# Halves of q and k turned 32 columns at a time, four side by side, in an attention and mixture-of-experts layer

## The chip, the cores and the metric

The kernel runs on one core of a Trainium2 chip. The metric is the device time of the program in microseconds; lower is better. Engines are named as the profile names them: PE is TensorE, DVE is VectorE, ACT is ScalarE, POOL is GpSimd, SP is SyncE, which only issues DMAs here.

## The reference

The input is x, 8 sequences of 512 tokens of 256 features. One layer is computed:

```python
x = layernorm(x + attention(x))
x = layernorm(x + ffn(x))

# attention: 16 heads of 16
qkv = x @ w_qkv.T                       # q, k, v
q, k = rms_norm(q) * q_w, rms_norm(k) * k_w
q, k = rope(q, k)                       # halves of each head rotated by cos, sin
attn = softmax(causal(q @ k.T) * 16 ** -0.5)
out = (attn @ v) @ w_proj.T

# ffn: a shared expert and the best 2 of 8 experts, 256 -> 1024 -> 256
normed = rms_norm(x) * norm_weight
shared = relu(normed @ sw1 + sb1) @ sw2 + sb2
routed = sum over the best two of w_e * (relu(normed @ ew1[e] + eb1[e]) @ ew2[e] + eb2[e])
```

## The kernel before

Each engine runs its own program, in order; semaphores are all that ties them together. The attention half is one long list of steps `g` from -40 to 209, the same for all engines: a job of batch `c` (one sequence) stands at step 20 c plus an offset from a table at the top of the file (`QK`, `ROPE`, `QN`, `TR`, `V`, `AV`, `NAT`, `PROJ` and so on), and the first two batches have offsets of their own (`OPENING`). Within a step each engine takes its jobs in the order in which its function `step` lists them. So in any stretch of 20 steps the scores of batch c run beside the preparation of q and k of batch c + 2 and the projection, norms and routing of batch c - 1. Below, "position 6 of a batch" is a step with g = 6 modulo 20, and "position 106" is g = 106. A tile is 128 tokens; a batch has four.

Products of two 32-bit values are made of 16-bit pieces: a value is a high part and a low part. For the scores each head's 16 columns of q stand in the contraction as high, low, high, low and those of k as high, low, low, high, 64 rows in all, so that one product of 64 rows gives all four pairs. The path of one tile of q and k is:

- TensorE makes q and k (L1681, position `QK`) and ScalarE copies them and their squares (L885, L888).
- GpSimd's `swap` (L696, L699) and VectorE's `rope` and `summed` (L1153, L1168) rotate them; VectorE's `normed` scales them into `qn` (L1183, position `QN`).
- One position later GpSimd's `nat_high` writes the high part into `nat` (L707); for the first batch ScalarE does it (`first_high`, L893). Two positions after `QN` VectorE's `nat_low` writes the low part (L1193).
- Three positions after `QN` GpSimd's `nat_twice` copies the two halves a second time, straight for q (L714) and with its parts swapped for k (L715), each as 256 words of 32 bits.
- At position `TR` (6, 10, 14 and 18 of a batch for tiles 0 to 3) TensorE's `stacked` turns the 64 columns of two heads at once: 8 turns of 128 columns for q into bank `ma` (L1691), 8 for k into bank `mc` (L1697). A turn is a matmul with the identity as the moving operand, 128 columns. ScalarE copies each bank into `stk` (L982, L985), from which the scores are made.

TensorE's order within a step is: scores and causal masks of two units (L1642, L1655), on even positions; `stacked`; `QK`; `V`; `NAT`, the attended rows turned back, tile t at positions 4, 6, 8, 10 (L1806); `AT` at 12 and 16 (L1706); `PROJ`, the projection, at 14 and 18 (L1818); `XN`, `LG`, `RANK`, the router's parts; `AV`, the pv products, at 1, 6, 11 and 16 (L1668). The pv products are already 32 columns wide and four side by side, each in a quarter of the array's columns. The scores use 64 rows, all else the full array.

`NAT` and `PROJ` share the bank `mb`: tile t + 1 of `NAT` waits for VectorE's L1202, which reads tile t out of it, and `PROJ` waits for `aT`, ScalarE's copy of the turned rows (L1003). VectorE's `added` reads the projection (L1220), makes the variance, and GpSimd's `norms` waits for that (L723). GpSimd also issues the scatters, indirect DMAs that write rows to DRAM by expert (L740, offsets `SPACED`). The next batch's x is split into high and low parts by ScalarE at position `SPLIT_X` (L1020) and VectorE one position later (L1452).

Of the kernel before, what the change touches and what calls it, by code (L numbers as in the profile page):

```python
# [8 lines left out]
ACT = mybir.ActivationFunctionType  # L9
AX = mybir.AxisListType  # L10
F32 = mybir.dt.float32
F16 = mybir.dt.float16
# [5 lines left out]
NB, T, D = 8, 512, 256  # L18
NH, HD = 16, 16
# [61 lines left out]
QN = (-20, -18, -12, -10)  # L81
TR = (-14, -10, -6, -2)
# [15 lines left out]
SPACED = (58, 60, 62, 66)  # L98
# [3 lines left out]
SPLIT_X = (-33,)  # L102
# [42 lines left out]
def due(offsets, g):  # L145

    return [(c, i) for i in range(len(offsets)) for c in range(NB) if position(offsets, c, i) == g]
# [99 lines left out]
def program(nc, a, S, keep):  # L247

    with ExitStack() as ctx:
# [80 lines left out]
        ma = ps("ma", T)  # L330
# [3 lines left out]
    with ExitStack() as ctx:  # L334
# [81 lines left out]
        def halves(n):  # L416

            if n in (2, 3):
                return prob[:, 1, n - 2, 0:1024].bitcast(F16).rearrange("p (k h d) -> p k h d", k=2, h=NH)
            return nat[:, n % 2]  # L420

        def halves_words(n):

            if n in (2, 3):
                return prob[:, 1, n - 2, 0:1024].rearrange("p (k h d) -> p k h d", k=2, h=NH)
            return nat[:].bitcast(F32)[:, n % 2]

# [47 lines left out]
        with nc.Block() as block:  # L475
# [176 lines left out]
            def _(pool):  # L652
# [56 lines left out]

                def nat_twice(n):  # L710

                    pool.wait_ge(S("nat_lo"), n + 1)
                    q, k = halves_words(n)[:, 0], halves_words(n)[:, 1]
                    pool.tensor_copy(q[:, :, HD:2 * HD], q[:, :, 0:HD]).then_inc(S("nat_ready"), 1)  # L714
                    pool.tensor_copy(k[:, :, HD:2 * HD].rearrange("p h (s d) -> p h s d", s=2),  # L715
                                     k[:, :, 0:HD].rearrange("p h (s d) -> p h s d", s=2)[:, :, ::-1, :]
                                     ).then_inc(S("nat_ready"), 1)
# [53 lines left out]
                def step(g):  # L771
                    for c, t in due(QN, g - 3):
                        nat_twice(4 * c + t)
# [62 lines left out]
            def _(act):  # L836
# [53 lines left out]
                def first_high(n):  # L890

                    act.wait_ge(S("qn_done"), n + 1)
                    act.activation(halves(n)[:, :, :, 0:HD].rearrange("p k h d -> p (k h) d"),  # L893
                                   qn[:, n % 2, :].rearrange("p (h d) -> p h d", d=HD), ACT.Copy).then_inc(S("nat_hi"), 1)

# [721 lines left out]
            def _(pe):  # L1617
# [67 lines left out]
                def stacked(c, t):  # L1685

                    n = 4 * c + t
                    pe.wait_ge(S("nat_ready"), 2 * (n + 1))
                    pe.wait_ge(S("ma_free"), NTH["tq", c, t])
                    for i in range(8):  # L1690
                        last = pe.transpose(ma[:, 64 * i:64 * i + 64].bitcast(F16),  # L1691
                                            halves(n)[:, 0, 2 * i:2 * i + 2, :].rearrange("p h d -> p (h d)"), ident_h[:])
                    last.then_inc(S("tq_done"), 1)
                    if NTH["tk", c, t]:
                        pe.wait_ge(S("mc_free"), NTH["tk", c, t])
                    for i in range(8):
                        last = pe.transpose(mc[:, 64 * i:64 * i + 64].bitcast(F16),  # L1697
                                            halves(n)[:, 1, 2 * i:2 * i + 2, :].rearrange("p h d -> p (h d)"), ident_h[:])
                    last.then_inc(S("tk_done"), 1)
# [77 lines left out]
                def step(g):  # L1777
# [9 lines left out]
                    for c, t in due(TR, g):  # L1787
                        stacked(c, t)
# [44 lines left out]
                    for c, _ in due(RANK, g):  # L1833
# [12 lines left out]
                        last.then_inc(S("rank_done"), 1)  # L1846
                    for c, i in due(AV, g):
                        attended(c, i)
# [188 lines left out]
```

## Time and profile before

| | |
|---|---|
| time, median of 3 runs | 947.77 us (946.87 to 948.3) |
| the profiled execution | 947.38 us, its span 945.6 us |
| PE busy | 882.1 us, 93% of the span |
| ACT busy | 614.4 us, 65% |
| DVE busy | 583.0 us, 62% |
| POOL busy | 438.7 us, 46% |
| mean granted clock of PE | 0.98 of full |
| L714, 28 copies in `nat` between 36 and 330 us | 20.9 us, mean 747 ns |
| L715, 28 copies in `nat` between 36 and 330 us | 14.4 us, mean 515 ns |

Positions 0, 20, 40, ... 140 begin at 36.13, 80.81, 122.59, 163.71, 205.44, 249.40, 290.64 and 328.70 us, read off the start of the first scores of each batch. Busy time is the union of an engine's instructions; "idle before" is the time in which the engine had nothing to run, with the instruction that ended it. The ends of matmuls are modelled, so a matmul of 128 columns is shown as 0.22 us though the next one starts some 0.06 us after it: in a row of eight the start of the next group tells the pace. Durations in the rows are of one profiled execution.

### The profile page before, as it was taken

Reading aid. Unit: us, or ns where it says so; the run is one execution under the profiler, and the core shown is the slowest. Engines: PE = TensorE matmul, PEld = TensorE weight load, DVE = VectorE, ACT = ScalarE, POOL = GpSimd, SP = SyncE. Lnnn points to the kernel's source line nnn. Section 1 sums busy time; section 2 is a strip of 40 time slices with the busy share of each in tenths; the row PEclk is TensorE's granted clock in tenths of the full one; section 3 lists DMA queues with packets and bytes.
Section 4 is the critical chain, followed back from the end, with each engine's and each line's share of the span. In section 5 each row is a group of like instructions: output and inputs, shape, how many; then the busy total and the mean of one; then the engine's idle time right before and its main releaser. Section 6 shows DMA issues by size and latency. Waiting matters only on the chain.

```text
span 945.6 us, 26104 instructions
## 1 busy us (share of the span) xinstructions
PE 882.1 (93%) x9049; PEld 699.2 (74%) x9050; DVE 583.0 (62%) x1206; ACT 614.4 (65%) x1061; POOL 438.7 (46%) x602
## 2 busy tenths in 40 slices
PE   3778999998999989999999999999999999999997
PEld 1444556565655646888889989989899989898886
DVE  8664778998888747784444444454444432437986
ACT  4678889887987866442656655556655454666774
POOL 5352555878777646572135444343434344421321
PEclk8799999999999999999999999999999999999999
DMA  5112242425312156567882122121212111238751
GB/s 177 68 68 68 68 146 90 139 100 184 108 70 75 61 181 217 210 209 268 273 283 78 52 62 69 54 67 52 72 45 79 46 58 47 70 114 286 233 168 55
DMA packets 68705, 112.76 MB, mean 119 GB/s; under 512 B 7728, under 2 KB 46000, under 8 KB 68496
## 3 DMA queue, kind: packets, MB, share of 16 engines
q1 hardware_dynamic: 51248, 77.32, 24.8%
q10 hardware_dynamic: 10896, 16.40, 5.8%
q0 software_dynamic: 6480, 17.97, 5.2%
q8 instruction: 50, 0.82, 0.4%
q14 instruction: 31, 0.25, 0.1%
HBM read 66.58 MB, written 45.08 MB: 118 GB/s over the span
## 4 chain that ended last, share of the span: by engine, by line
PE 64%; POOL 11%; ACT 9%; issue 9%; DVE 3%; DMA 2%; another core or an unknown queue 1%; ACTq 0%; DVEq 0%; POOLq 0%; SPq 0%
PE yb L1903 24%; PE hb L1884 24%; ACT prob L871 4%; PE pv_bank L1668 4%; PE hb L1734 3%; POOL xg_rows L740 2%; PE slot L1642 1%; PE tr L1754 1%; POOL rsum L699 1%; PE ma L1681 1%; POOL rsum L696 1%; POOL vv L723 1%; POOL nat L707 1%; PE yb L1771 1%
## 5 line engine op out<-in xcount | busy, mean ns | idle before, releaser
L1043 ACT ACTIVATE hf<-hb,b 128x256 f32<-128x256 f32 (+1 forms) x392 | 154.8, 453 | 201.1 <-PE hb L1884 182.5
L1884 PE MATMUL hb<-xgT,wts 128*128 128x256 f16 (+1 forms) x1872 | 213.3, 263 | 1.5 <-ACT hf L1043 1.3
L1903 PE MATMUL yb<-wts,hh 128*128 x1704 | 210.5, 273 | 0.7 <-DVE hh L1472 0.6
L1472 DVE TENSOR_TENSOR hh<-hf,hh 128x1024 f16<-128x1024 f32 (+1 forms) x98 | 119.9, 1227 | 132.9 <-ACT hh L1048 105.0
L1884 PEld LDWEIGHTS hb<-xgT,wts 128*128 x1872 | 181.2, 98 | 20.7 <-ACT hf L1043 1.1
L806 POOL DMA_INDIRECT y_tok<-yb,dest x71 | 77.7, 1095 | 229.0 <-DVE yb L1484 212.2
L1903 PEld LDWEIGHTS yb<-wts,hh 128*128 128x128 f16 x1704 | 166.4, 98 | 19.4 <-DVE hh L1472 0.9
L871 ACT ACTIVATE prob<-slot 128x1024 f32<-128x1024 f32 x160 | 156.1, 1037 | 31.9 <-PE slot L1655 29.9
L1048 ACT ACTIVATE hh<-hf 128x1024 f16<-128x1024 f32 (+1 forms) x98 | 97.6, 996 | 3.1
L740 POOL DMA_INDIRECT xg_rows<-xnh,sl_i x64 | 78.3, 1224 | 15.5 <-issue 13.2
L1484 DVE SCALAR_TENSOR_TENSOR yb<-yb,b2bc 128x512 f32<-128x512 f32 (+1 forms) x39 | 25.1, 643 | 85.2 <-PE yb L1903 84.0
L1668 PE MATMUL pv_bank<-prob,vst 128*32 128x512 f32 (+3 forms) x1024 | 76.6, 440 | 0.5 <-ACT prob L871 0.5
L1642 PE MATMUL slot<-stk 64*128 64x128 f16 (+3 forms) x512 | 53.6, 303 | 23.2 <-ACT prob L871 16.5
L1681 PE MATMUL ma<-wqkv,xTh 128*128 128x256 f16 (+1 forms) x348 | 65.0, 333 | 9.1 <-ACT raw L888 3.8
L1668 PEld LDWEIGHTS pv_bank<-prob,vst 128*32 128x32 f32 x1024 | 30.0, 110 | 45.4 <-issue 35.5
L1642 PEld LDWEIGHTS slot<-stk 64*128 64x128 f16 x512 | 18.0, 94 | 49.6 <-ACT prob L871 27.3
L1681 PEld LDWEIGHTS ma<-wqkv,xTh 128*128 128x128 f16 x348 | 34.0, 100 | 27.5 <-issue 6.3
L1884 PE MATMUL hb<-xgT,wts_s 128*128 128x256 f16 x480 | 54.0, 273 | 0.0
L1903 PE MATMUL yb<-wts_s,hh 128*128 128x256 f16 x456 | 51.3, 273 | 0.0
L1884 PEld LDWEIGHTS hb<-xgT,wts_s 128*128 128x128 f16 x480 | 47.0, 98 | 5.4
L723 POOL TENSOR_TENSOR vv<-vv,keep_mhalf 128x4 f32<-128x4 f32 x16 | 21.5, 1345 | 62.2 <-DVE vv L1239 62.2
L1903 PEld LDWEIGHTS yb<-wts_s,hh 128*128 128x128 f16 x456 | 44.6, 98 | 5.2
(250 smaller groups left out, 1441.6 us busy)
## 6 DMA issues: line engine op xcount, KB each, us to landing
wts<-in_w_all SPq DMA_DIRECT2D x23, 512.0 KB
wts<-y_tok SPq DMA_DIRECT2D x32, 256.0 KB, 4.9
xg<-xg_rows ACTq DMA_DIRECT2D x30, 264.0 KB, 2.7
stage<-in_w_all SPq DMA_DIRECT2D x12, 512.0 KB
w_split<-chunk_hl SPq DMA_DIRECT2D x12, 512.0 KB
xTf<-in_xT SPq DMA_DIRECT2D x8, 512.0 KB, 4.4
xin<-in_x SPq DMA_DIRECT2D x8, 512.0 KB, 4.1
resid<-y SPq DMA_DIRECT2D x16, 256.0 KB
```

Source lines behind the costliest of these rows:

```text
L723: pool.tensor_tensor(vv[:, pair(u), 4:6], vv[:, pair(u), 0:2], mhalf[:].unsqueeze(1).broadcast_to([P, 2, 2]), ALU.pow).then_inc(S("norms_r ...
L740: pool.indirect_dma_start(a["xg_rows"], bass.IndirectOffsetOnAxis(ap=sl_i[:, c % 2, t, k:k + 1], axis=0), xnh[:, c % 2, t, :], None).then_ ...
L806: pool.indirect_dma_start(a["y_tok"], bass.IndirectOffsetOnAxis(ap=dest[:, slot, j:j + 1], axis=0), yb[:, par, j, :], None).then_inc(S(f"y ...
L871: act.activation(dst, src, ACT.Exp, scale=ATT_SCALE).then_inc(S("exp_done"), 1)
L1043: act.activation(hf[:, c, 0:size], hb[c // 2][:, (c % 2) * TT:(c % 2) * TT + size], ACT.Relu, bias=bias, scale=1.0 / WS).then_inc(S("relu_ ...
L1048: act.activation(hh[:, par, 0, cs, 0:size], hf[:, cs, 0:size], ACT.Copy).then_inc(S("h_hi"), 1)
L1472: dve.tensor_tensor(hh[:, par, 1, cs, 0:size], hf[:, cs, 0:size], hh[:, par, 0, cs, 0:size], ALU.subtract).then_inc(S("h_lo"), 1)
L1642: pe.matmul(slot[:, 512 * x + col:512 * x + col + T - P * j], stk[rows, par, 1, pr, P * j:P * j + P], stk[rows, par, 0, pr, P * j:T], star ...
L1668: last = pe.matmul(pv_bank[32 * r:32 * r + 32, P * j:T], vst[:, c % 2, j, 4 * g + r, :], prob[:, g % 2, r, SEG[j]:SEG[j] + T - P * j], sta ...
L1681: last = pe.matmul(out, xTh[:, c % 2, x, k, P * t:P * t + P], wqkv[:, y, k, cols], start=(n == 0), stop=(n == len(pieces) - 1))
L1884: ins = pe.matmul(hb[hc // 2][:, (hc % 2) * TT:(hc % 2) * TT + size], weights(e, c, w, hc * P, P), xgT[:, par, x * DC + c, 0:size], start= ...
L1903: ins = pe.matmul(bank, hh[:, par, x, hc, P * j:P * j + P], weights(e, DC + hc * D // CH, w, hc * D % CH, D), start=(n == 0), stop=(n == H ...
```

## The change

`nat_twice` goes. Instead the high part of k is written a second time, behind its low part, so that a head of k holds high, low, high: by GpSimd behind `nat_high`, by ScalarE behind `first_high` for the first batch. `stacked` no longer turns 64 doubled columns of two heads at once but 32 columns at a time into a quarter of the partitions, four such matmuls to a block: for q high and low of a head, twice; for k columns 0 to 31 (high, low) and 16 to 47 (low, high). It is moved in TensorE's step from behind the masks to ahead of the pv products. The third scatter of a batch's first four goes from offset 62 to 64, and the split of x from -33 to -34.

```diff
--- before.py
+++ after.py
@@ -95,11 +95,11 @@
 RANK = (56,)
 SCATTER = (58, 59, 61, 63)
 SCATTER_2 = (64, 66, 67, 68)
-SPACED = (58, 60, 62, 66)
+SPACED = (58, 60, 64, 66)
 SPACED_2 = (67, 68, 70, 72)
 STORE = (39, 43)
 STORE_XT = (43, 49)
-SPLIT_X = (-33,)
+SPLIT_X = (-34,)
 LOAD_XIN = (20,)
 LOAD_XT = (-51,)
 UNITS = tuple(range(NPOS))
@@ -419,12 +419,6 @@
                 return prob[:, 1, n - 2, 0:1024].bitcast(F16).rearrange("p (k h d) -> p k h d", k=2, h=NH)
             return nat[:, n % 2]
 
-        def halves_words(n):
-
-            if n in (2, 3):
-                return prob[:, 1, n - 2, 0:1024].rearrange("p (k h d) -> p k h d", k=2, h=NH)
-            return nat[:].bitcast(F32)[:, n % 2]
-
         def rotated(n):
 
             return prob[:, 1, n, 0:2 * D] if n in (2, 3) else rsum[:, n % 2, :]
@@ -706,15 +700,8 @@
                     pool.wait_ge(S("tk_done"), n - 1)
                     pool.tensor_copy(nat[:, n % 2, :, :, 0:HD].rearrange("p k h d -> p (k h) d"),
                                      qn[:, n % 2, :].rearrange("p (h d) -> p h d", d=HD)).then_inc(S("nat_hi"), 1)
-
-                def nat_twice(n):
-
-                    pool.wait_ge(S("nat_lo"), n + 1)
-                    q, k = halves_words(n)[:, 0], halves_words(n)[:, 1]
-                    pool.tensor_copy(q[:, :, HD:2 * HD], q[:, :, 0:HD]).then_inc(S("nat_ready"), 1)
-                    pool.tensor_copy(k[:, :, HD:2 * HD].rearrange("p h (s d) -> p h s d", s=2),
-                                     k[:, :, 0:HD].rearrange("p h (s d) -> p h s d", s=2)[:, :, ::-1, :]
-                                     ).then_inc(S("nat_ready"), 1)
+                    pool.tensor_copy(nat[:, n % 2, 1, :, 2 * HD:3 * HD],
+                                     qn[:, n % 2, D:2 * D].rearrange("p (h d) -> p h d", d=HD)).then_inc(S("nat_again"), 1)
 
                 def norms(c, u):
 
@@ -769,8 +756,6 @@
                                            ).then_inc(S("x1_done"), 1)
 
                 def step(g):
-                    for c, t in due(QN, g - 3):
-                        nat_twice(4 * c + t)
                     for c, t in due(QN, g - 1):
                         if c >= 1:
                             nat_high(4 * c + t)
@@ -892,6 +877,9 @@
                     act.wait_ge(S("qn_done"), n + 1)
                     act.activation(halves(n)[:, :, :, 0:HD].rearrange("p k h d -> p (k h) d"),
                                    qn[:, n % 2, :].rearrange("p (h d) -> p h d", d=HD), ACT.Copy).then_inc(S("nat_hi"), 1)
+                    act.activation(halves(n)[:, 1, :, 2 * HD:3 * HD],
+                                   qn[:, n % 2, D:2 * D].rearrange("p (h d) -> p h d", d=HD), ACT.Copy
+                                   ).then_inc(S("nat_again"), 1)
 
                 def roots(c, u):
 
@@ -1685,17 +1673,24 @@
                 def stacked(c, t):
 
                     n = 4 * c + t
-                    pe.wait_ge(S("nat_ready"), 2 * (n + 1))
+                    pe.wait_ge(S("nat_lo"), n + 1)
+                    pe.wait_ge(S("nat_again"), n + 1)
                     pe.wait_ge(S("ma_free"), NTH["tq", c, t])
+
+                    def turned(bank, i, r, rows):
+
+                        return pe.matmul(bank[32 * r:32 * r + 32, 64 * i:64 * i + 64].bitcast(F16), rows, ident_h[:],
+                                         is_transpose=True)
+
                     for i in range(8):
-                        last = pe.transpose(ma[:, 64 * i:64 * i + 64].bitcast(F16),
-                                            halves(n)[:, 0, 2 * i:2 * i + 2, :].rearrange("p h d -> p (h d)"), ident_h[:])
+                        for r in range(4):
+                            last = turned(ma, i, r, halves(n)[:, 0, 2 * i + r // 2, 0:2 * HD])
                     last.then_inc(S("tq_done"), 1)
                     if NTH["tk", c, t]:
                         pe.wait_ge(S("mc_free"), NTH["tk", c, t])
                     for i in range(8):
-                        last = pe.transpose(mc[:, 64 * i:64 * i + 64].bitcast(F16),
-                                            halves(n)[:, 1, 2 * i:2 * i + 2, :].rearrange("p h d -> p (h d)"), ident_h[:])
+                        for r in range(4):
+                            last = turned(mc, i, r, halves(n)[:, 1, 2 * i + r // 2, HD * (r % 2):HD * (r % 2) + 2 * HD])
                     last.then_inc(S("tk_done"), 1)
 
                 def rows_turned(bank, rows, u):
@@ -1784,8 +1779,6 @@
                                 scores(c, k)
                             for k in (p, p + 1):
                                 masked(k)
-                    for c, t in due(TR, g):
-                        stacked(c, t)
                     for c, t in due(QK, g):
                         if c >= 1:
                             pe.wait_ge(S("xT_lo"), c + NT)
@@ -1844,6 +1837,8 @@
                                              msum[:, i, :].unsqueeze(1).broadcast_to([P, NT, NE]),
                                              start=False, stop=(i == NT - 1), skip_group_check=True)
                         last.then_inc(S("rank_done"), 1)
+                    for c, t in due(TR, g):
+                        stacked(c, t)
                     for c, i in due(AV, g):
                         attended(c, i)
                     for kind, m, q in early_due(g):
```

## Rows read from the trace of the kernel before

**Rows 1.** Busy time of each engine in 249.40 to 290.60 us (windows), with counts.

```profile
249.40:290.60 41.20, 38.96 (x456) 24.12 (x456) 36.48 (x94) 35.29 (x56) 30.81 (x37) 1.00 0.27 94
```

**Rows 2.** Waits of TensorE, 80.8 to 328.7 us: us in total, times, longest.

```profile
PE slot L1642 <- ACT prob L871: 6.9, 16, 1.2
PE ma L1691 <- POOL nat L715: 4.1, 4, 1.4
```

**Rows 3.** Timeline of TensorE, positions 100 to 120: start, length, line, [idle before <-releaser].

```profile
261.53 0.62 PE L1691 MATMUL ma<-keep_ident,nat 128*128 128x128 f16 x8 [0.58 <-POOL nat L715]
261.99 0.61 PE L1697 MATMUL mc<-keep_ident,nat 128*128 128x128 f16 x8
...
268.81 0.39 PE L1642 MATMUL slot<-stk 64*128 64x512 f16 x2 [0.20 <-ACT prob L871]
269.72 0.39 PE L1642 MATMUL slot<-stk 64*128 64x128 f16 x4 [0.52 <-ACT prob L871]
...
270.39 0.61 PE L1691 MATMUL ma<-keep_ident,nat 128*128 128x128 f16 x8
...
278.66 0.61 PE L1691 MATMUL ma<-keep_ident,nat 128*128 128x128 f16 x8
...
287.64 0.61 PE L1691 MATMUL ma<-keep_ident,nat 128*128 128x128 f16 x8
```

**Rows 4.** Timeline of TensorE, the turn of tile 0 in the two batches before.

```profile
176.61 0.62 PE L1691 MATMUL ma<-keep_ident,nat 128*128 128x128 f16 x8 [1.35 <-POOL nat L715]
...
218.36 0.62 PE L1691 MATMUL ma<-keep_ident,nat 128*128 128x128 f16 x8 [1.38 <-POOL nat L715]
```

**Rows 5.** Copies on GpSimd, 36 to 330 us: busy us, mean ns | idle before.

```profile
L714 POOL COPY nat<-nat 128x256 f32<-128x256 f32 x28 | 20.9, 747 | 25.5 <-DVE nat L1193 25.3 <-issue 0.2
...
L715 POOL COPY nat<-nat 128x256 f32<-128x256 f32 x28 | 14.4, 515 | 0.0
```

**Rows 6.** Timeline of VectorE, positions 101 to 110.

```profile
257.46 1.89 DVE L1193 TENSOR_TENSOR nat<-qn,nat 128x512 f16<-128x512 f32 x1 [0.28 <-POOL nat L707]
...
261.20 0.42 DVE L1202 TENSOR_TENSOR an<-mb,rcp 128x256 f32<-128x256 f32 x1
...
267.42 0.69 DVE L1168 TENSOR_TENSOR rsum<-rot,rsum 128x512 f32<-128x512 f32 x1 [0.85 <-POOL rsum L699]
...
270.82 0.42 DVE L1202 TENSOR_TENSOR an<-mb,rcp 128x256 f32<-128x256 f32 x1
```

**Rows 7.** Timeline of VectorE beside the two turns of rows 4.

```profile
176.62 0.42 DVE L1202 TENSOR_TENSOR an<-mb,rcp 128x256 f32<-128x256 f32 x1
...
217.70 0.42 DVE L1202 TENSOR_TENSOR an<-mb,rcp 128x256 f32<-128x256 f32 x1
```

**Rows 8.** Timeline of ScalarE, positions 107 to 120.

```profile
266.80 1.04 ACT L1020 ACTIVATE xTh<-xTf 128x1024 f16<-128x1024 f32 x1
...
278.36 0.65 ACT L1003 ACTIVATE aT<-mb 128x512 f32<-128x512 f32 x1
...
289.92 0.62 ACT L985 ACTIVATE stk<-mc 128x512 f32<-128x512 f32 x1
```

**Rows 9.** VectorE groups, 36 to 330 us: busy us, mean ns | idle before.

```profile
L1193 DVE TENSOR_TENSOR nat<-qn,nat 128x512 f16<-128x512 f32 x28 | 23.1, 825 | 8.1 <-POOL nat L707 7.9
...
L1452 DVE TENSOR_TENSOR xTh<-xTf,xTh 128x1024 f16<-128x1024 f32 x6 | 7.4, 1226 | 0.2
```

**Rows 10.** Timeline of TensorE's weight loads in and behind the pv products.

```profile
220.26 0.13 PEld L1668 LDWEIGHTS pv_bank<-prob,vst 128*32 128x32 f32 x4 [0.30 <-issue]
220.69 0.13 PEld L1668 LDWEIGHTS pv_bank<-prob,vst 128*32 128x32 f32 x4 [0.30 <-issue]
...
222.09 0.33 PEld L1642 LDWEIGHTS slot<-stk 64*128 64x128 f16 x8 [0.20 <-issue]
```

**Rows 11.** The page, part 5: the weight loads of the pv products: busy us, mean ns.

```profile
L1668 PEld LDWEIGHTS pv_bank<-prob,vst 128*32 128x32 f32 x1024 | 30.0, 110 | 45.4 <-issue 35.5
```

**Rows 12.** TensorE's sequencer at line L1804, 261 to 263 us.

```profile
L1804 PEldq EVENT_SEMAPHORE  x1: 51/51/51, 261.7 to 261.7; - x1
```

## The prediction, made blind

> **What bounds the kernel now.** I read the page first, then the same stretch four times over: TensorE's waits in it, and the timelines of TensorE, VectorE, ScalarE and GpSimd side by side. The page's slices show TensorE at nine tenths through the second half of the span: the feed-forward half, behind the attention, is matmuls back to back, and nothing that the change touches runs there. So the change can act only in the attention half, and whatever it wins or loses by position 140 (328.7 us) is carried to the end. There a batch lasts some 41 us, and in the one that I follow, positions 100 to 119, TensorE is busy 38.96 of 41.20 us, ScalarE 35.29, VectorE 36.48, GpSimd 30.81 [rows 1]. The reader is to see that four engines run nearly full, with TensorE nearest its limit: a wait removed on GpSimd is worth at most what TensorE waits.
>
> TensorE's own waits from position 20 to 140 are the budget of the argument [rows 2]: 4.1 us in 4 waits for GpSimd's doubling copies, 6.9 us in 16 waits for an exponential to free a scores bank. The first kind sits at one place, the turn of tile 0 at position 6 of a batch (0.58 us in the batch that I follow [rows 3]; 1.35 and 1.38 two and one batches earlier [rows 4]). At position 10 the scores wait 0.20 and 0.52 us [rows 3].
>
> **The copies removed.** GpSimd loses 32 pairs, of 747 and 515 ns on average, and gains 28 copies of a quarter of q and k's values; the nearest row is the second removed copy, 515 ns, which I take, so a batch has 4 x (1.26 - 0.52) = 3.0 us less GpSimd work [rows 5]. That alone is worth nothing: what counts is who waits. For tile 0 that is TensorE, 4.1 us in all [rows 2]. For VectorE it is the sum of the next tile (0.85 us [rows 6]), late because the copies stood ahead of GpSimd's swap.
>
> **What takes the wait's place.** The turn no longer stands ahead of the attended rows' turns (L1806) and of the projection (L1818), but behind them. At position 6 the attended tile 1 needs the bank from VectorE's L1202 on tile 0. That ends at 261.62, while the doubling copies let TensorE go at 261.53 [rows 3, 6]: the new wait ends 0.09 us later than the old one. In the two batches of [rows 4, 7] L1202 ends at 177.04 and 218.12 against 176.61 and 218.36. From the end of the scores TensorE would then wait 1.35 + 0.43 = 1.8, 1.38 - 0.24 = 1.1, 0.58 + 0.09 = 0.7, and in batch 6, which has the remaining 0.8 of the 4.1 us, some 0.9: 4.5 us in place of 4.1. Behind the waiting instruction TensorE has the turn, the pv products and the next scores queued, and ScalarE's exponentials wait for those. Against it, the projection is no longer behind the turn at positions 14 and 18, so VectorE's sums, GpSimd's norms and the tile's start on VectorE come earlier, by up to the 0.9 us that two half turns take (8 turns in 0.46 us [rows 3]). GpSimd is not idle before it, so I credit 0.5 us in each of four batches: 2.0 us.
>
> **The split of x one position earlier.** ScalarE's 1.04 us (L1020 at 266.80 [rows 8]) stood behind the copy that waits for the pv products and ahead of the exponentials of position 8; it now runs while ScalarE would wait for pv. It can take at most 1.04 us from the waits of position 10; in the batch followed there are 0.20 + 0.52 = 0.72, and five batches have such a split: 3.6 us (bounds 0 and 5.2). But VectorE's half (L1452, 1226 ns [rows 9]) moves too, from behind to ahead of its L1202 on tile 2, which ended at 271.24 where TensorE began the turn of tile 1 at 270.39 [rows 3, 6]. With the attended turn first, TensorE wants that bank at 270.39 - 0.72 = 269.67 and gets it at 271.24 + 1.23 - 0.85 (the wait of VectorE that goes) - 0.5 = 271.12: 1.4 us. In the other four batches VectorE is further ahead; I take 0.3 each: 2.6 us in all (bounds 0 and 5 x 1.4 = 7.0).
>
> **The turns moved behind the projection.** At position 14 the turn began at 278.66, and the projection, which now comes first, needs ScalarE's aT, done at 279.01 [rows 3, 8]. The turn used to cover this: 0.35 us and some 0.03 for the semaphore, six times: 2.3 us. At position 18 the scores of the next batch wait for ScalarE's copy of the turned k, begun at 289.92 [rows 8]. The turn began at 287.64 [rows 3]. Now 12 matmuls of 256 columns go first, 1.37 us at 57 ns for 128; with a change of array shape (0.1, below), two half turns (0.92) and the tail of the last (0.16) k is turned at 290.2, some 0.2 us after ScalarE wanted it: six times 0.2, 1.2 us. Position 14 also gets a change between full-width and 32-column matmuls that was not there. The load behind pv starts after a gap of 0.20 us [rows 10]; between nothing and that I take 0.1, six times: 0.6 us. Positions 6 and 10 have pv next, so none is added.
>
> **The turns themselves.** 16 turns of 128 columns become 64 of 32, four side by side. Two things could make them dearer. First the pace of a group of four: in pv the loads of a set of four stand 0.43 us apart (220.26, 220.69) for 512 fp32 columns, that is 0.107 for 128, and a 16-bit turn streams in half that time: 8 turns in 0.46 us, 57 ns each [rows 3, 10]. Four loads of 110 ns are over in 0.13 us, so they start within 0.02 us [rows 10, 11]. So a group of four should take the time of one full turn and I charge nothing; the other bound is a whole load of 110 ns [rows 11] for each group in place of 57 ns: 53 ns more x 16 groups x 28 tiles = 24 us. Second the instructions: 96 more a tile, 3,072 in all. After the wait ended at 261.53, TensorE's sequencer was past all 32 instructions of a turn by 261.7 [rows 3, 12], some 5 ns each, while the new turns need 128 in 0.9 us, 7 ns each: hidden. The Trainium skill has a figure against the change: "TensorE: Matmul & The Clock Gate", section LDWEIGHTS, gives the load as columns / 1.2 ns, 27 ns for 32 columns, 107 ns if the four of a group followed one another; its section Back-to-back issue gap has a floor of some 25 ns for a matmul, 100 ns for four. By either a tile costs about 0.8 us more, an estimate; pv's loads and matmuls, 0.02 us for four, disagree [rows 10].
>
> **The opening.** The tiles of the first batch wait for the copies too, but the last of them waits for VectorE's work on tiles 2 and 3, which does not change, and ScalarE gets four more copies ahead of its own copies of the turned tiles. I set it at 0, between one pair of copies won and as much lost, 1.3 us [rows 5]. The scatter moved from position 62 to 64 goes behind the high part of tile 1 in GpSimd's queue, and its DMA with it; its rows are read only after the attention half, and with the copies gone nothing of TensorE waits behind it: 0.
>
> **Sum.** Won: 4.1 + 3.6 + 2.0 = 9.7. Lost: 4.5 + 2.6 + 2.3 + 1.2 + 0.6 = 11.2. Net 1.5 us slower. The profiled execution took 947.38 us (945.6 of span), 0.4 under the median of the runs, 947.77; I add the sum to the median: **949.3 us**. This measurement can tell some 0.2%, 1.9 us, from no change.
>
> **Rivals.** (A) *VectorE is freed and the new waits vanish: faster.* Its L1193 on tile 0 lasted 1.89 us beside GpSimd, against 825 ns on average [rows 6, 9]. If less GpSimd work gives it 1.2 us back, L1202 comes that much earlier, the wait at position 6 falls from 4.5 - 2.0 = 2.5 to nothing and that at position 10 from 2.6 to nothing: 1.5 - 5.1 = -3.6 us, 944.2, and with the upper bound of the split of x, 5.2 for 3.6, 942.6. For it: every term on VectorE is short of its limit by a microsecond or less. Against: the removed copies ran mostly when VectorE's durations were normal. It decides as soon as VectorE gains 0.6 us a batch. (B) *VectorE's chain gets longer: slower.* The new copy stands on GpSimd straight ahead of the swap, where L1193 was held 1.2 us. If it is held 0.5 us longer, the credit of 2.0 goes and both waits grow, 6 x 0.4: 1.5 + 2.0 + 2.4 = 5.9 us, 953.7. It decides if L1193 at position 2 lasts over 2 us. (C) *The loads of a group are not hidden:* 24 us more, 975; against it speaks pv. The skill's figures would give the same, 0.8 x 28 = 22 us, an estimate.
>
> **Chances.** Forecast (946 to 952) 0.36, of it 0.06 faster, 0.20 the same, 0.10 slower; A 0.32, faster; B 0.22, of it 0.04 the same; C 0.10, slower. So faster 0.38, same 0.24, slower 0.38. The range leaves out C and the far ends of A: 941 to 959; the forecast's own is 946 to 952.
>
> **What would show it.** Right: L1691's waits for GpSimd gone; L1806 at position 6 waiting for VectorE, L1818 at position 14 for ScalarE, some 0.4 us; a half turn of 32 matmuls in 0.45 to 0.5 us; position 20 to 140 lasting 248 to 251 us against 247.9. Wrong: those waits at zero (A), L1193 at 2 us or more (B), a half turn of 0.8 us or more (C), or a wait on the turn itself for VectorE's low part, which I have at nothing.

## The result and the profile after

The kernel after takes 953.58 us (median of 5 runs, 951.71 to 954.25) against 947.77 (946.87 to 948.3): 1.0051 of before, 95% interval 1.0031 to 1.0071, so slower, by 4.8 us at that ratio. Its profiled execution took 953.96 us against 947.38. The 6.6 us between the two lie where the prediction looked: from position 20 to 140 the attention half lasts 253.5 us (82.53 to 336.00) in place of 247.9, 1.7 us more come up to position 20, and behind position 140 it is 0.7 us less.

The batches from 164.60, from 207.94 and from 252.00 us, the last to be read against [rows 1] (start:end, length, busy us of PE, PEld, DVE, ACT, POOL, granted clock):

```profile
252.00:297.20 45.20, 40.98 (x648) 25.47 (x649) 38.16 (x99) 35.68 (x56) 28.10 (x36) 0.96 0.24 82
207.94:252.00 44.06, 40.57 (x648) 25.30 (x649) 38.68 (x91) 37.45 (x58) 29.93 (x34) 0.96 0.38 125
164.60:207.94 43.34, 39.42 (x649) 24.38 (x650) 39.09 (x100) 36.53 (x57) 29.67 (x35) 1.00 0.39 127
```

GpSimd is relieved as the change wants (28.10 us busy for 30.81), and yet the batch followed in the prediction takes 4.0 us longer: TensorE is busy 2.0 us more, at 0.96 of its clock, and idle 2.0 us more. VectorE is busy 1.7 us more, though its program is the same.

Waits of TensorE, 82.5 to 336 us, to be read against [rows 2]:

```profile
PE slot L1630 <- ACT prob L856: 6.3, 12, 1.6
PE mb L1799 <- DVE an L1190: 4.5, 5, 1.8
PE slot L1630 <- ACT stk L970: 3.4, 4, 0.9
PE mb L1811 <- ACT aT L991: 2.4, 6, 1.1
PE slot L1630 <- ACT stk L973: 1.8, 1, 1.8
PE mc L1682 <- issue: 0.9, 2, 0.5
PE slot L1630 <- issue: 0.8, 1, 0.8
```

The wait for the doubling copies is gone; the attended rows wait for VectorE and the projection for ScalarE instead, as forecast. The scores at the six batch starts from position 20 to 120 wait 6.0 us in all (3.4 and 1.8 for ScalarE's copies of the turned rows, 0.8 at 164.60 for nothing that the profile names) in place of 5.1. Timeline of TensorE in the batch of [rows 3]:

```profile
263.71 0.63 PE L1799 MATMUL mb<-ident_f,raw 128*128 128x128 f32 x4 [0.16 <-DVE an L1190]
264.27 0.63 PE L1682 MATMUL ma<-keep_ident,nat 128*32 128x128 f16 x32
264.73 0.82 PE L1682 MATMUL mc<-keep_ident,nat 128*32 128x128 f16 x32
...
274.39 1.08 PE L1799 MATMUL mb<-ident_f,raw 128*128 128x128 f32 x4 [1.82 <-DVE an L1190]
275.41 1.04 PE L1682 MATMUL ma<-keep_ident,nat 128*32 128x128 f16 x32
276.24 1.07 PE L1682 MATMUL mc<-keep_ident,nat 128*32 128x128 f16 x32
...
284.34 1.48 PE L1811 MATMUL mb<-wproj,aT 128*128 128x256 f16 x12 [0.27 <-ACT aT L991]
285.76 0.63 PE L1682 MATMUL ma<-keep_ident,nat 128*32 128x128 f16 x32
286.21 0.62 PE L1682 MATMUL mc<-keep_ident,nat 128*32 128x128 f16 x32
286.77 0.61 PE L1630 MATMUL slot<-stk 64*128 64x128 f16 x6
```

32 narrow turns stand 0.46 us apart (264.27, 264.73), as 8 wide ones did. Behind the wait of 1.82 us at position 10 the half turns take 0.83 and 0.85: the clock has fallen, as the two windows below show, one over that place and one ten microseconds earlier (granted clock third from the right):

```profile
274.00:277.40 3.40, 3.01 (x72) 2.58 (x76) 3.19 (x9) 1.09 (x2) 1.56 (x3) 0.51 0.09 30
264.00:267.40 3.40, 3.40 (x98) 2.06 (x97) 3.30 (x4) 3.40 (x6) 3.21 (x4) 1.00 0.14 43
```

0.51 is the 1.2 GHz level, 1.00 the 2.4 GHz one; TensorE had been idle 1.8 us just before. VectorE shows what made that wait; compare [rows 6]:

```profile
259.14 2.22 DVE L1181 TENSOR_TENSOR nat<-qn,nat 128x512 f16<-128x512 f32 x1 [0.28 <-POOL nat L701]
...
272.39 1.22 DVE L1440 TENSOR_TENSOR xTh<-xTf,xTh 128x1024 f16<-128x1024 f32 x1
...
273.82 0.42 DVE L1190 TENSOR_TENSOR an<-mb,rcp 128x256 f32<-128x256 f32 x1
```

VectorE's half of the split of x now stands ahead of L1190 on tile 2, so L1190 ends at 274.24, and the low part, beside GpSimd's second copy and its swap, lasts 2.22 us in place of 1.89.

What was not forecast is at position 6 and after. In the batch before the one above, TensorE, then ScalarE, then GpSimd:

```profile
220.93 2.33 PE L1656 MATMUL pv_bank<-prob,vst 128*32 128x512 f32 x32
...
228.47 0.39 PE L1630 MATMUL slot<-stk 64*128 64x512 f16 x2 [1.62 <-ACT prob L856]
...
231.31 1.04 PE L1682 MATMUL ma<-keep_ident,nat 128*32 128x128 f16 x32
```

```profile
222.19 1.14 ACT L1008 ACTIVATE xTh<-xTf 128x1024 f16<-128x1024 f32 x1
225.15 0.60 ACT L861 ACTIVATE raw<-pv_bank 128x512 f32<-128x512 f32 x1 [1.81 <-remote]
...
227.41 1.92 ACT L856 ACTIVATE prob<-slot 128x1024 f32<-128x1024 f32 x2
```

```profile
221.65 1.01 POOL L727 DMA_INDIRECT xg_rows<-xnh,sl_i  x1 [0.17 <-issue]
222.96 0.96 POOL L727 DMA_INDIRECT xg_rows<-xnh,sl_i  x1 [0.30 <-issue]
224.23 1.02 POOL L727 DMA_INDIRECT xg_rows<-xnh,sl_i  x1 [0.30 <-issue]
```

The pv products of position 6 end at 223.26. ScalarE's copy of them, L861, waits for nothing else, and yet starts at 225.15, as the third of three scatters on GpSimd ends (225.25). The profile names no instruction of this core as the releaser ("remote"). The trace's record of the semaphore says the same: its update stands at 225.12, 1.87 us behind the end that the profile gives the pv products. The masks behind them, by their rows over at 224.12 and 224.34, are released at 225.92, while TensorE goes on starting a matmul every 0.11 us. The exponentials queued behind the copy are then late, the scores of position 10 wait 1.62 us, and the next turns run at half clock. In the kernel before the scatters started 2.1 to 2.2 us behind the pv products.

What this costs can't be read off this batch, since the kernel before waits and falls to half clock at the same place. Its TensorE, and a window there (granted clock third from the right):

```profile
226.59 0.39 PE L1642 MATMUL slot<-stk 64*128 64x512 f16 x2 [1.15 <-ACT prob L871]
```

```profile
228.50:231.90 3.40, 3.40 (x26) 2.10 (x26) 3.37 (x5) 2.72 (x4) 3.23 (x2) 0.50 0.34 122
```

The batch lasts 44.06 us after and 43.96 before. Of the 5.6 us that positions 20 to 140 grew by, 4.0 lie in the batch from 252.00 us, with the wait of 1.82 us for VectorE and the half clock behind it, which the kernel before doesn't have there.

### The profile page after: what moved, and what is told of

It is laid out like the page before. It is cut to its first block, busy times and chain, and to the rows that moved or that the text cites. A ratio compares the mean times of both kernels' runs of the same rounds, so it can differ in the third digit from the quotient of the medians.

```text
span 952.2 us, 29144 instructions
## 1 busy us (share of the span) xinstructions
PE 887.7 (93%) x10585; PEld 701.9 (74%) x10586; DVE 587.1 (62%) x1206; ACT 616.6 (65%) x1065; POOL 410.4 (43%) x566
## 4 chain that ended last, share of the span: by engine, by line
PE 68%; ACT 10%; DVE 7%; issue 6%; POOL 4%; DMA 2%; another core or an unknown queue 1%; ACTq 0%; DVEq 0%; SPq 0%; POOLq 0%
PE yb L1898 24%; PE hb L1879 24%; PE pv_bank L1656 5%; ACT prob L856 5%; PE hb L1729 3%; PE slot L1630 2%; PE ma L1669 2%; PE slot L1643 2%; PE mb L1811 1%; PE tr L1749 1%; DMA rs<-resid 1%; PE yb L1766 1%; PE ma L1682 1%; DVE nat L1181 1%
## 5 line engine op out<-in xcount | busy, mean ns | idle before, releaser
L727 POOL DMA_INDIRECT xg_rows<-xnh,sl_i x64 | 74.5, 1164 | 15.4 <-issue 12.8
L701 POOL CAST nat<-qn 128x512 f16<-128x512 f32 x28 | 22.9, 818 | 61.1 <-DVE qn L1171 58.2
```

The lines of the kernel that those rows point to most:

```text
L727: pool.indirect_dma_start(a["xg_rows"], bass.IndirectOffsetOnAxis(ap=sl_i[:, c % 2, t, k:k + 1], axis=0), xnh[:, c % 2, t, :], None).then_ ...
```

## The experiments

Twelve kernels, each timed in five rounds beside the kernel before on the same chip: e1 to e4 on one chip, f1 to f4 on a second, g1 to g4 on a third. Results are ratios to the kernel before of the same rounds, with 95% intervals; the quotient of two of them is known to some 0.2 to 0.35%. Five theories came up, three at first: O, the order of the turns costs; S, the earlier split pays; W, narrow turns cost (called P with f1 to f4); and later V, the second copy of k's high parts holds VectorE; C, the scatter's place matters. The first four kernels take away the order, the split, both, or everything else.

**e1, the turns ahead again.** The kernel after, with:

```
+                    for c, t in due(TR, g):
+                        stacked(c, t)
                     for c, t in due(QK, g):
...
-                    for c, t in due(TR, g):
-                        stacked(c, t)
                     for c, i in due(AV, g):
```

> The changed kernel with the turns back at their old place in TensorE's step (behind the masks, ahead of the attended rows' turns and the projection); 32-column turns, no doubling copies, the split of x and the scatter as changed. Theory O (the order costs: TensorE stands at the attended turn for VectorE and at the projection for ScalarE's aT): the 4.5 and 2.4 us of those waits go, so it is 5 to 8 us faster than the changed kernel, 945.5 to 948.5, and the waits for L1190 and L991 vanish from TensorE's list. Theory S (the split of x is what costs, by VectorE's half ahead of L1190): within 2 us of the changed kernel, 952 to 955. Theory W (the 32-column turns themselves are dearer than they look): within 2 us of the changed kernel too.

**e2, the split at -33** (`-SPLIT_X = (-34,)`, `+SPLIT_X = (-33,)` in the kernel after).

> The changed kernel with the split of x back at -33, nothing else. Theory S: VectorE's 1.23 us is again behind its L1190 on tile 2, the wait of 1.82 us at position 10 falls under 0.7, 3 to 5 us faster than the changed kernel, 949 to 951. Theory O: the waits for L1190 shrink but the exponentials of position 8 come 1 us later, within 2 us of the changed kernel, 952 to 955.

**e3, both of these edits.**

> Both taken back: the turns ahead and the split of x at -33; what is left of the change is the 32-column turns, the copies gone and the scatter at 64. Theory W: still 3 us or more slower than the kernel before, over 951. Theories O and S: nothing waits for the doubling copies (4.1 us) any more and no new wait is added, so 2 to 4 us faster than the kernel before, 944 to 946.

**e4, only the order.** The kernel before, wide turns and doubling copies, with the first diff the other way round.

> The kernel before, with full-width turns and the doubling copies, and only the turns moved behind the projection, ahead of the pv products. Theory O: 4 to 8 us slower than the kernel before, 952 to 956, with TensorE's waits for L1202 and aT. Theories S and W: within 1.5 us of the kernel before.

Measured: e1 1.0071 (1.0045 to 1.0097), e2 1.0063 (1.0043 to 1.0083), e3 1.0130 (1.0095 to 1.0164), e4 0.9979 (0.9961 to 0.9997). So theory O falls: the order alone is worth 2 us (e4), and with narrow turns and without the doubling copies it is worth 0.67% (e3 over e2). The split is nearly neutral beside pv (e2) and pays 0.6% where the turns stand ahead (e3 over e1). What costs is in the turns or the copies. Theories O and S forecast 944 to 946 us for e3; it is the slowest kernel of all, 960.97.

**f1, narrow turns over doubled columns.** e4 with:

```
                     for i in range(8):
-                        last = pe.transpose(ma[:, 64 * i:64 * i + 64].bitcast(F16), ...)
+                        for r in range(4):
+                            last = turned(ma, i, r, halves(n)[:, 0, 2 * i + r // 2, 2 * HD * (r % 2):2 * HD * (r % 2) + 2 * HD])
...
```

and the same for k into `mc`.

> e4_only_moved (turns behind the projection, split of x and scatter as before) with the turns 32 columns wide, but taken from the doubled layout: GpSimd's doubling copies stay and there is no second high copy. It tells the width alone. Theory P (the narrow turns cost on TensorE: two more changes of array shape a batch, more instructions, a lower clock): 3 to 8 us slower than e4_only_moved. Theory V (the cost lies in GpSimd's new copy, which stands where VectorE writes the low part, 165 ns longer on average in the changed kernel): within 2 us of e4_only_moved.

**f2, the second copy later.** e2, with GpSimd's second copy taken out of `nat_high` into a function of its own, `nat_again`, and:

```
                 def step(g):
+                    for c, t in due(QN, g - 3):
+                        if c >= 1:
+                            nat_again(4 * c + t)
```

> e2_split_later (the changed kernel with the split of x at -33) with GpSimd's second copy of k's high part two positions later, where the doubling copies stood. Theory V: VectorE's low part is no longer held beside it (1022 ns on average back to some 860), 4 us or more faster than e2_split_later. Theory P: within 2 us of e2_split_later.

**f3, the scatter back.** e2 with `SPACED = (58, 60, 62, 66)`.

> e2_split_later with the scatter back at offset 62 from 64. A third theory, C: the scatter at 64 stands ahead of the swap of tile 2 and makes it late, with it VectorE's sum and all behind: then 3 us or more faster than e2_split_later. Theories P and V: within 2 us of it.

**f4, one copy more.** e4 with the second high copy beside the doubling copies.

> e4_only_moved with full-width turns and the doubling copies, and GpSimd's second copy of k's high part added behind the first (it is overwritten by the doubling copy later, so nothing is changed in the output). Theory V: the low part lasts over 1000 ns on average and it is 3 to 7 us slower than e4_only_moved. Theory P: within 2 us of e4_only_moved; in both GpSimd has 0.4 to 0.6 us more a tile.

Measured: f1 1.0015 (0.9997 to 1.0033), f2 1.0039 (1.0021 to 1.0058), f3 1.0115 (1.0087 to 1.0144), f4 0.9996 (0.9980 to 1.0012). The narrow turns cost 0.36% (f1 over e4), as theory P had it. The copy as an extra costs 0.17%, though it lengthens the low parts to 945 ns from 830 on average; moved later (f2 under e2) it gives 0.24% back; both are within the intervals and under what theory V forecast. Theory C went the other way round: scatter 64 saves 0.5% (e2 under f3), where every theory had f3 within 2 us of e2, or faster. And there is a gap: f1 and f3 differ only in the copies, GpSimd's work from position 0 to 140 is 167.1 us in f3 against 185.4, and f3 is 1.0% slower.

The last four kernels are the fourth corner of the square {wide, narrow} x {doubled, second copy}, a kernel half way, and two that start from e4.

**g1, wide turns with the second copy.** f3 with the turns of before:

```
-                        for r in range(4):
-                            last = turned(ma, i, r, ...)
+                        q = halves(n)[:, 0, 2 * i:2 * i + 2, :].rearrange("p h d -> p (h d)")
+                        last = pe.transpose(ma[:, 64 * i:64 * i + 64].bitcast(F16), q, ident_h[:])
```

It leaves the mixed products of high and low parts out of the scores, since the columns that would hold the doubled halves are zero; GpSimd writes these zeros once at the start.

> The fourth corner of a square: turns wide or narrow, by doubling copies or by the second copy of k's high parts, all with the turns beside pv, the split of x at -33 and the scatter at 62. Three corners are measured: wide and doubled 0.9979 of before, narrow and doubled 1.0015, narrow and second copy 1.0115. This one has the second copy and turns 128 columns at a time again, which read columns that are zero in place of the doubled ones, so what it computes of q and k is wrong; GpSimd zeroes those columns once at the start. Theory W, the narrow turns' instructions on TensorE are late in supply and hold up its semaphores where turns and pv stand side by side (in the kernel after, pv_done at position 6 comes 0.65 to 1.87 us after the end that its records give, with nothing else released in between): without them those late updates go, and the time falls to 0.996 to 1.000 of before (944 to 949 us), 12 to 15 us under the narrow one. Theory G, the second copy holds VectorE up (its low parts take 965 to 1022 ns in the place of 859) and that is what costs the 9.5 us between narrow doubled and narrow second copy: the time stays at 1.006 to 1.010 (955 to 958 us). If the two simply add: 1.0115 less 0.0036 is 1.008, 957 us.

**g2, only k narrow** (g1 with k's loop of four; the same products are left out, since q's doubled columns are zero).

> As the one before, q turned wide (reading zeros in the doubled columns, so its result is wrong), k turned 32 columns at a time: half of the extra instructions. Theory W: if the supply runs out only past some density, this is near the wide one (0.997 to 1.002 of before) and pv_done at position 6 is on time; if each extra instruction costs alike, halfway between the wide one and 1.0115. Theory G: as the wide one, 1.006 to 1.010, since the copies are the same.

**g3, e4 with** `SPACED = (58, 60, 64, 66)`.

> The kernel before with the turns beside pv and the third scatter at 64. The scatter at 62 cost 0.5% in the narrow kernel (5 us). If that holds for the wide one too, 0.992 to 0.994 of before (941 to 943 us); if it mattered only because GpSimd's second copy stands there, 0.998, as the turns moved alone.

**g4, g3 with** `SPLIT_X = (-34,)`.

> The kernel before with all of the change but the narrow turns and the copies: turns beside pv, the third scatter at 64, the split of x at -34. The split was worth 0.1% (unclear) beside pv and 0.6% ahead. Expected 0.991 to 0.997 of before (940 to 946 us), under both kernels; it would be at or over 0.998 if scatter and split are worth something only beside the second copy.

Measured: g1 1.0067 (1.0054 to 1.0081), g2 1.0077 (1.0063 to 1.0090), g3 0.9956 (0.9941 to 0.9971), g4 0.9990 (0.9980 to 0.9999). The square, in per cent of before:

| | doubling copies | second copy |
|---|---|---|
| wide | e4 -0.21 | g1 +0.67 |
| narrow | f1 +0.15 | f3 +1.15 |

Taking the doubling copies away costs 0.88% and 1.00% (known to 0.23 and 0.34), narrowing the turns 0.36% and 0.48% (to 0.25 and 0.32); within that the two add. g3 came between its two forecasts, and g4 was slower than the 0.991 to 0.997 that was expected. The idea behind W here, that the late release of the pv products came of the narrow turns' instructions, fell with g1: with wide turns it is late by as much. Theory G's number for g1 (1.006 to 1.010) came true, but not its cause: in f4 the low parts take 945 ns on average, in g1 933, and f4 costs 0.17%. Here is g1 at position 6, TensorE, ScalarE and GpSimd:

```profile
223.06 2.36 PE L1662 MATMUL pv_bank<-prob,vst 128*32 128x512 f32 x32
...
231.42 0.39 PE L1636 MATMUL slot<-stk 64*128 64x512 f16 x2 [1.97 <-ACT prob L862]
...
234.35 1.06 PE L1690 MATMUL ma<-keep_ident,nat 128*128 128x128 f16 x8
```

```profile
227.08 0.60 ACT L867 ACTIVATE raw<-pv_bank 128x512 f32<-128x512 f32 x1 [3.20 <-remote]
```

```profile
223.50 1.03 POOL L733 DMA_INDIRECT xg_rows<-xnh,sl_i  x1 [0.17 <-issue]
224.84 0.97 POOL L733 DMA_INDIRECT xg_rows<-xnh,sl_i  x1 [0.30 <-issue]
226.11 1.02 POOL L733 DMA_INDIRECT xg_rows<-xnh,sl_i  x1 [0.30 <-issue]
```

And e4 at the same place, in the same order:

```profile
219.56 2.36 PE L1668 MATMUL pv_bank<-prob,vst 128*32 128x512 f32 x32
```

```profile
221.99 0.60 ACT L876 ACTIVATE raw<-pv_bank 128x512 f32<-128x512 f32 x1 [1.41 <-PE pv_bank L1668]
```

```profile
221.37 0.93 POOL L714 COPY nat<-nat 128x256 f32<-128x256 f32 x1 [2.66 <-DVE nat L1193]
...
224.16 1.54 POOL L740 DMA_INDIRECT xg_rows<-xnh,sl_i  x1 [0.16 <-issue]
```

In e4 GpSimd waits 2.66 us for VectorE's low parts before it doubles them, so its scatters start at 224.16, 2.2 us behind the end of the pv products (221.92); ScalarE takes those at once. In g1 no doubling copy waits, GpSimd reaches the scatters 2 us ahead of the pv products' end (225.42), and ScalarE starts at 227.08, when the third scatter ends (227.13). The same in all four batches from position 60 on, in us from the end of the pv products of position 6, batch by batch: where the first scatter near them starts, and how late ScalarE's copy of them is.

```
          first scatter starts            ScalarE's copy late by
before     2.19,  2.15,  2.14,  2.14      0
e4         1.60,  2.24,  1.90,  1.85      0
f1         1.64,  1.61,  1.93,  1.61      0
after     -0.66, -1.61, -0.59, -1.98      0.65, 1.87, 0.73, 1.54
g1        -1.96, -1.91, -1.96, -1.96      1.58, 1.64, 1.53, 1.52
f3        -1.94, -1.72, -1.94, -1.95      2.40, 1.84, 1.66, 1.63
f2        -1.06, -1.44, -1.06, -2.23      1.03, 1.41, 1.00, 2.24
e3        -2.85, -3.40, -2.86, -2.87      0, 1.31, 0, 0
```

With the copies doubled GpSimd comes to the scatters behind the pv products, without them in their midst. In eleven of the twelve late cases of after, g1 and f3 ScalarE started within 0.25 us of the end of a scatter; in f2 in one of four.

The loss of time lies in these four batches. From position 60 to 140 g1's profile is 9.2 us longer than e4's and f3's 9.0 longer than f1's, of 9.8 and 9.5 from position 20; in the two batches before, in which nothing is scattered yet, the missing copies cost 0.6 us. That they scatter is not all that is new in the four: the other work of the routing stands there too. Part of the loss is the clock: its mean over all timed runs is 0.985 in e4 and in f1 and 0.980 in g1 and in f3.

e3 does not fit. There the turns stand ahead, the first scatter starts 2.9 to 3.4 us ahead of the pv products' end, and the pv products are released on time in three batches of four. Still e3 is 1.3% slower than the kernel before, and its profile is longer by 1.8, 3.0, 1.2 and 1.3 us in the same four batches and by 3.3 us behind position 140. The narrow turns account for 3.4 to 4.6 us of its 12, and its scatter at 64 for none. So late pv releases can hardly be the whole price of the missing copies.

## Why the prediction came out as it did

The time lies in the stated range (941 to 959), but over the forecast's own 946 to 952, and the sign leaned on nothing: 0.38 on each side. Positions 20 to 140 lasted 253.5 us where 248 to 251 was to show the mechanism right. It is in good part luck that the time came so near: the experiments put 8.3 to 9.5 us on the copies' removal, which the prediction had at nothing beyond TensorE's waits, and against it 2 to 5 us saved by the scatter, also at 0. Of the sum, net 1.5 us slower against 4.8 measured, step by step:

- **Won 4.1, GpSimd's wait gone:** right. **The turns at no charge for the loads of a group (rival C's 24 us):** C is refuted, 0.46 us for a half turn, as forecast from pv's loads (its sum gives 973 us, not 975). With it falls the prediction's estimate of 0.8 us more a tile, worked out of two figures of the Trainium skill ("TensorE: Matmul & The Clock Gate", LDWEIGHTS and Back-to-back issue gap) as if the four of a group followed one another. But 0.6 us for the turns' changes of array shape was mis-sized: narrowing costs 0.36 to 0.48%, 3.4 to 4.6 us. Much of it is seen in the profiles of f1 and e4. At the batch starts from position 20 to 140 the scores wait 8.4 us in f1 and 6.5 in e4; at three of them f1 waits for nothing that the profile names. Behind the longest of these (1.92 us, 207.80) f1 runs at half clock for a while, e4 nowhere from position 20 on. And the instructions were not all hidden: at 314.91 and 315.78 TensorE pauses 0.51 and 0.38 us in the midst of k's turns (in the changed kernel 0.42 and 0.47, at 206.59 and 295.90), which it never does where k's turns are wide. Waits of TensorE in f1, 36 to 338 us:

```profile
PE slot L1642 <- issue: 4.2, 3, 1.9
```

  Half of the extra instructions, g2, cost 0.10% of the 0.48, known to 0.19, so whether the price goes by their number can't be told. What makes TensorE wait there stays open.
- **Lost 4.5 at position 6:** over-sized. L1190 made TensorE wait there 1.07 and 0.16 us. **Lost 2.6 at position 10:** the right place, 0.77, 0.70 and 1.82 us, 3.3 in all, and half clock stood behind the last. g3 and g4 show the mechanism by itself, in the kernel with the doubling copies. Waits of TensorE from 36 to 338 us, g3 and then g4:

```profile
PE mb L1804 <- DVE an L1202: 1.8, 3, 0.9
```

```profile
PE slot L1642 <- ACT prob L871: 7.9, 12, 2.7
PE mb L1804 <- DVE an L1202: 6.3, 6, 2.1
```

  The split one position earlier takes 3.7 us off the waits for exponentials (11.6 in g3), 3.6 being forecast, and puts 4.5 on those for VectorE: 0.34% slower in sum. In the changed kernel it is 0.1% faster, which is no measurable difference; there ScalarE has the gap before the late pv copy to put it in (222.19 above).
- **Lost 2.3 at position 14:** 2.4 measured, in six waits. **Lost 1.2 at position 18:** 0.9 measured at the batch starts, and the two pauses in k's turns, 0.9, stand there too. **Credit 2.0 for the projection ahead:** too small or a matter of the clock. In e4 the wait for GpSimd's copies is gone too (4.1), waits for VectorE (2.9) and for aT (2.4) stand in its place, 1.2 us more, and yet the kernel is 2.0 us faster: 3.2 to be explained. In the profiles e4 wins 1.4 and 1.9 us in just the two batches in which the kernel before has a stretch at half clock (from 81.75 and 228.53 us) and e4 none. Whether the order brings that about was not tried.
- **The opening, 0 within 1.3:** 0.5 us slower at position 0.
- **Rival B (953.7)** gave the measured time with a mechanism of the right kind and a small share: L1181 at position 2 lasts 2.22 us, over its bound of 2, and the mean of all low parts rises from 828 to 985 ns. But f4 and f2 price it at 0.17 to 0.24%, about 2 us, neither clear of its interval. **Rival A** is refuted: VectorE gained nothing, its busy time in the batch followed is 1.7 us more.
- **What failed** is the step on GpSimd's work: the copies' removal "alone is worth nothing: what counts is who waits", with the scatter, "nothing of TensorE waits behind it: 0". I asked who waits for GpSimd, not what GpSimd starts sooner. Freed of the wait for the low parts (23.7 us idle ahead of L714 in the kernel before, 82 to 336 us), its scatters slide 3 to 4 us forward across the pv products of position 6, whose release comes late. By their absence the copies cost 0.9 to 1.0%; how much of that goes through the late releases is not measured, and e3 speaks against all of it. The scatter at 64, priced at 0, saves 0.23% beside the doubling copies (g3 under e4, at the edge of its interval) and 0.52% beside the second copy.

The chain from the late release to the time is read in the timelines: ScalarE's copy, the exponentials, scores of position 10, half clock. That a scatter in progress holds TensorE's release up is inferred from the coincidence of its end with ScalarE's start. Since the ends of matmuls are modelled in the profile (the Trainium skill, "Perfetto Trace Analysis", section Tensor Engine Instruction, says so, and that a matmul's release goes out only when its bank has taken all of its writes), the trace can't tell a release that was held up from pv products that really ended late. No run kept the doubling copies and moved the scatters forward by themselves, and the hold is not a strict rule: many other releases of TensorE during scatters came at once (in the changed kernel at 301.88, 0.04 us behind pv products that end in the midst of a scatter), one in f3 came 0.6 us after a scatter's end, and one in the kernel before, at 344.31, 1.4 us after one. What in the chip ties them was not tried. Another cause that goes with the missing copies is not ruled out, and e3 asks for one.

The version that beats both is g3, turns beside pv and the third scatter at 64, wide turns, doubling copies and the split left as they were: 944.43 us, 0.9956 (0.9941 to 0.9971), some 4.2 us under before.

## What to carry to other kernels

Taking work and a wait off an engine with slack can move everything queued behind it forward: look up what it starts then, above all DMAs that it issues itself, and what those lie across. A bundle of edits that comes out near zero may hold a real gain: undo or do each by itself, and fill all corners of a square where two could act together. When an operation moves from behind to ahead of an engine's critical instruction, count both engines' halves of it; here ScalarE's gain of 3.7 us and VectorE's loss of 4.5 were one edit.

## What the runs showed of the hardware

- Four matmuls of 32 columns side by side, each with its own load, run at the pace of one of 128: 32 in 0.46 us, each matmul 219 ns long in the profile in either width. Now and then there is a pause in a group, 0.38 to 0.51 us in the changed kernel and in f1.
- ScalarE's start on a bank whose last matmul had ended came 0.65 to 2.4 us late in twelve cases while GpSimd was issuing three scatters in a row, in eleven of them to within 0.25 us of a scatter's end. It is no rule: in other cases the release came at once.
- VectorE's two-operand subtraction of 128x512 takes 0.69 us at its shortest (263.93 us before) and 2.22 beside GpSimd's second copy and swap (259.14 us after); the mean of 24 is 828 ns before, 945 with the second copy added (f4), 985 after.
- Behind a wait of 1.6 to 2.0 us between full stretches TensorE had half clock, at that place or within 2 us behind it, in each of the three cases shown (half turns 0.83 to 0.86 us apart for 0.46), so such a wait can cost more than its length. It does not always: in f2 a wait of 1.97 us (227.44) had none behind it, and in the kernel before waits of 1.15 and 0.52 us (226.59 and 227.50) did.
